# Weight loads, weight conversions and the last product's scaling stand at other steps in a relational graph layer

## The chip, the cores and the metric

The kernel runs on one core of one Trainium2 chip. The time is the device time of one execution in microseconds; lower is better. Before the change it is 1454.06 us, the median of 3 runs (1453.46 to 1455.05).

## What is computed

Two relational graph convolutions over 1250 nodes with 768 features and 21250 edges of 8 relations, then a residual and a layer norm. Each convolution takes the mean of the source rows for every pair of node and relation, multiplies it by the relation's matrix, sums over the relations and adds a root product and a bias:

```python
def _rgcn_conv(x, src, dst, etype, W, root, b):
    seg = dst * num_rel + etype
    sums = segment_sum(x[src], seg)                  # per (node, relation)
    cnt = segment_sum(ones, seg)
    mean = (sums / maximum(cnt, 1.0)[:, None]).reshape(num_nodes, num_rel, -1)
    return einsum('nri,rio->no', mean, W) + x @ root + b

h = relu(_rgcn_conv(x, src, dst, etype, W1, root1, b1))
out = _layernorm(x + _rgcn_conv(h, src, dst, etype, W2, root2, b2))
```

## The kernel before

The kernel turns the order round: it multiplies first, y = h W_r for all nodes, and then gathers rows of y by edge and sums them by destination. Every fp32 operand is cut in two parts that TensorE takes, a rounded one ("high") and the rest ("low"), and a product is three matmuls: high by high, high by low, low by high.

There are 18 products, numbered 0 to 17 here as `q` in the code: 0 to 7 are the relations of layer 1, 8 is its root; 9 to 16 and 17 are those of layer 2. A product has 20 steps: column half h = 0 with ten tiles of 125 nodes, then h = 1 with the same ten. A step is 6 x 3 = 18 matmuls of 128x384 into one of four PSUM banks. Of a product that is stored, ScalarE copies the bank to one of four slots of `y_stage` (`stage_y`), SyncE issues two DMAs that store it to y in HBM (`store_y`), and the slot is free for step s + 4 once both have landed (`y_stored[s % BANKS]`).

A "sum" (`bucket`) adds up one tile of 125 nodes of one relation. Its two row tiles (in the last relation of a layer four, of which the last is folded in half) are gathered from y by GpSimd (`gather_tile`, into seven, later five slots of `raw`), ScalarE makes `g_high` of each (`high_of_tile`; four slots, so a tile waits until TensorE has used the tile four before it), VectorE makes `g_low` (`cut_low`) and the one-hot matrix of destinations (`mark`), TensorE multiplies (8 matmuls for a plain sum, 14 for one of four row tiles), and VectorE adds the result to `acc` (`add`).

Products 4, 5 and 6 go with sums of two relations each ("pairs of sums"), one sum behind nearly every step. Product 7 and those of layer 2 go with sums of one relation. The root products 8 and 17 are written by `finish`: their 20 steps stay in PSUM, and the sums of the last relation of the layer are added onto them in the same banks.

Weights come in halves. `load_unit(q, h)` is one DMA of 1152 KB by SyncE into the single buffer `w_raw`; it waits until the half before has been converted. `high_of_unit` is its conversion on ScalarE, `low_of_unit` that on VectorE (in the pair products in two pieces, by the table `in_parts`). Half 1 of product q is needed at step 10, half 0 of q + 1 at its step 0. At which step each engine does this is written out by hand in three places: `relation` (SyncE; loads behind the stores of steps 8 and 14), `matrix` of ScalarE (steps 1 and 11) and `matrix` of VectorE (the table `low_at`). Each engine works in the order written: what stands behind a waiting instruction waits too. At step s of ScalarE the sum's `g_high` come first, then `stage_y(s)`, then the conversion. The kernel has no scheduler.

`finish(1)`, the last product, also does the layer norm. For tile t VectorE makes mean and variance (`moments_of`), ScalarE the root (`deviation`), VectorE its reciprocal and the shift (`scale_of`), and ScalarE scales the rows (`norm`), which SyncE stores to `out`. The last tile is done in two halves (`last_bucket`, `last_moments`) and scaled by VectorE.

Of the kernel before, what the change touches and what calls it, by code (L numbers as in the profile page):

```python
# [8 lines left out]
def rgcn_residual_layernorm(nc, x, src, dst, etype, w_all, b1, b2, out):  # L9
# [23 lines left out]
    K = D // P  # L33
# [51 lines left out]
    with ctx:  # L85
# [305 lines left out]
        def _(sp):  # L391
# [20 lines left out]

            def relation(q, yc, r):
                for s in range(STEPS):
                    store_y(yc, r, s)
                    if isinstance(q, int) and q == TABLE_END and s == 3:
                        sp.wait_ge(flags_counted, 1)
                        sp.dma_start(inv_table.rearrange("(p k) o -> p (k o)", p=P), inv_count[:])\
                            .then_inc(inv_stored, 16)
                    if s == 8:  # L420
                        load_unit(q + 1, 0)
                    if s == 14:
                        load_unit(q + 1, 1)

# [36 lines left out]
            for q in range(1, ROOT1):  # L461
                relation(q, q, q)
                if q == TABLE_END:
                    sp.wait_ge(bucket_added, 2 + T)
                    sp.dma_start(bias[:], b2.rearrange("(o n) -> o n", o=1).to_broadcast([P, D]))\
                        .then_inc(bias_loaded, 16)
# [146 lines left out]
        def _(act):  # L613
# [41 lines left out]

            def matrix(q, yc, actions=lambda s: [], after=None):


                for s in range(STEPS):
                    for what, g, _, t in actions(s):  # L660
                        if what == "sum":
                            bucket(g, t)
                    stage_y(yc, STEPS * q + s, s, bank_of(s))
                    for what, turn, _, t in actions(s):
                        if what == "turn":
                            high_of_turn(turn, t)
                    if s == 1:
                        high_of_unit(q, 1)
                    if s == 11:
                        high_of_unit(q + 1, 0)  # L670
                    if after:
                        after(s)
# [39 lines left out]
            def finish(layer):  # L712
# [5 lines left out]
                for t in range(T):  # L718
                    if layer == 0 and t == T - 2:
                        high_of_unit(q + 1, 0, STEPS * q + FIRST_HALF)  # L720
                    if t + 1 < T:
                        bucket(g, t + 1)
                    if layer == 0:
                        relu(t)
                        if t:
                            high_of_turn(1, t - 1)
                    else:
                        deviation(t)
                        if t + 1 < T:
                            norm(t)  # L730

# [11 lines left out]
            for q in range(TABLE_END, ROOT1 - 1):  # L743
                matrix(q, q, pair_of(q))
            matrix(ROOT1 - 1, ROOT1 - 1, one_relation(R - 2, None))
            finish(0)
# [235 lines left out]
        def _(dve):  # L982
# [372 lines left out]
            def finish(layer):  # L1355
# [6 lines left out]
                for t in range(T):  # L1362
                    if layer == 0 and t == T - 2:
                        low_of_unit(unit(q + 1, 0), 0)
                    if t + 1 < T:
                        cut_low(g, t + 1, 0, 1)
                    if (layer, t) == (1, T - 1):
                        last_moments(g, t)
                        continue
                    add(g, R - 1, t)  # L1370
                    if t + 1 < T:
                        cut_low(g, t + 1, 1)
                    if layer:
                        moments_of(t)
                    if t + 2 < T:
                        mark(g, R - 1, t + 2)
                    if layer and t + 1 < T:
                        scale_of(t)
                    elif layer == 0 and t:
                        low_of_turn(1, t - 1)  # L1380
# [23 lines left out]

            in_parts = ((4, 0, K // 2), (7, K // 2, K), (13, 0, K // 2), (16, K // 2, K))
            for q in range(TABLE_END, ROOT1 - 1):
# [35 lines left out]
```

## Time and profile before

| | us |
|---|---|
| median of 3 runs | 1454.06 |
| the profiled execution | 1466.17 |
| its span in the trace | 1464.3 |
| TensorE busy | 1437.1 (98%) |
| VectorE busy | 927.6 (63%) |
| ScalarE busy | 573.1 (39%) |
| GpSimd busy | 559.0 (38%) |

The profiled execution lies 12.1 us above the median of the runs, and 1.9 us of it lie outside the span. The trace knows the engines as PE (TensorE matmul), PEld (its weight load), DVE (VectorE), ACT (ScalarE), POOL (GpSimd) and SP (SyncE). In brackets behind a row of the timeline stand the idle time of the engine just before it and what ended that. PE is nearly always busy, so what can be won is in its few gaps and at the two ends.

### The profile page before, as it was taken

The page shows a single profiled execution, that of the slowest core. Times are in us where ns is not written, and L with a number is a line of the kernel's source. Part 1 is how long each engine was busy: PE and PEld are TensorE (multiplying, and loading weights), DVE is VectorE, ACT ScalarE, POOL GpSimd, SP SyncE. Part 2 cuts the span into 40 slices and gives each one's busy share as a digit, 9 for nine tenths or more (in the row PEclk, how much of TensorE's full clock was granted, in tenths as well). Part 3 has the DMA queues.
Part 4 walks back from the last instruction along what each step waited for, and adds up shares of the span by engine and source line. Part 5 has one row for each costly group of instructions (what it writes and reads, how often), then busy time and mean ns, then how long its engine had stood idle before and what let it go on. Part 6 is the DMA issues. An engine that isn't in the chain of part 4 may idle for free.

```text
span 1464.3 us, 23621 instructions
## 1 busy us (share of the span) xinstructions
PE 1437.1 (98%) x8715; PEld 1419.6 (97%) x8715; DVE 927.6 (63%) x1475; ACT 573.1 (39%) x805; POOL 559.0 (38%) x437
## 2 busy tenths in 40 slices
PE   8999999999999899999999999999999999999997
PEld 8999999999999899999999999999999999999996
DVE  7899999857777577456771154545454454444677
ACT  4222334335444444344552233333343333433454
POOL 0000000066777686425535232434242424243552
PEclk9999999999999999999999999999999999999998
DMA  6414321358877776664463465646464656656454
GB/s 195 152 60 127 96 72 47 106 183 267 254 211 227 227 229 191 212 200 149 136 189 103 148 211 168 210 144 218 142 211 156 199 177 184 194 171 213 119 169 123
DMA packets 112523, 248.58 MB, mean 170 GB/s; under 512 B 19617, under 2 KB 87768, under 8 KB 112446
## 3 DMA queue, kind: packets, MB, share of 16 engines
q0 software_dynamic: 30880, 134.67, 31.1%
q1 hardware_dynamic: 81566, 112.88, 24.1%
q8 instruction: 48, 0.79, 0.2%
q14 instruction: 29, 0.24, 0.0%
HBM read 192.77 MB, written 65.49 MB: 176 GB/s over the span
## 4 chain that ended last, share of the span: by engine, by line
PE 89%; DVE 6%; issue 3%; ACT 1%; DMA 1%; SPq 0%; ACTq 0%; POOLq 0%
PE prod L767 70%; PE agg L809 14%; DVE g_low L1029 2%; PE agg L904 2%; PE agg L767 2%; PE prod L809 1%; PE agg L758 1%; DVE g_high L1029 1%; ACT g_high L628 1%; DVE acc L1046 1%; DVE g_low L1033 1%; DMA x_rows<-in_x 0%; PE agg L907 0%; DVE stats L1401 0%; DMA raw<-y,bucket_index 0%
## 5 line engine op out<-in xcount | busy, mean ns | idle before, releaser
L767 PE MATMUL prod<-w_high,h_high 128*128 128x384 f32 x2064 | 693.5, 336 | 0.0
L767 PE MATMUL prod<-w_high,h_low 128*128 128x384 f32 x2064 | 690.4, 335 | 0.0
L767 PE MATMUL prod<-w_low,h_high 128*128 128x384 f32 x2064 | 690.1, 334 | 0.0
L519 POOL DMA_INDIRECT raw<-y,bucket_index x310 | 410.5, 1324 | 538.5 <-DVE g_low L1033 220.1
L653 ACT ACTIVATE y_stage<-prod 128x384 f32<-128x384 f32 x320 | 157.7, 493 | 781.6 <-PE prod L767 631.1
L1033 DVE TENSOR_TENSOR g_low<-raw,g_high 128x768 fp32r<-128x768 f32 x240 | 220.4, 956 | 370.6 <-ACT g_high L631 312.4
L767 PEld LDWEIGHTS prod<-w_high,h_high 128*128 128x128 f32 x2064 | 388.1, 188 | 0.1
L767 PEld LDWEIGHTS prod<-w_low,h_high 128*128 128x128 f32 x2064 | 388.0, 188 | 0.0
L767 PEld LDWEIGHTS prod<-w_high,h_low 128*128 128x128 f32 x2064 | 387.8, 188 | 0.0
L631 ACT ACTIVATE g_high<-raw 128x768 fp32r<-128x768 f32 x240 | 189.9, 839 | 1.9 <-DMA raw<-y,bucket_index 1.5
L809 PE MATMUL agg<-g_high,one_hot 128*128 128x384 f32 x616 | 159.8, 340 | 10.1 <-DVE g_low L1033 7.6
L809 PE MATMUL agg<-g_low,one_hot 128*128 128x384 f32 x602 | 153.5, 336 | 0.0
L1049 DVE SCALAR_TENSOR_TENSOR acc<-agg,inv_count,acc 128x768 f32<-128x768 f32 x130 | 131.7, 1013 | 11.4 <-PE agg L809 7.6
L809 PEld LDWEIGHTS agg<-g_high,one_hot 128*128 128x128 f32 x616 | 109.8, 189 | 16.3 <-issue 13.7
L995 DVE TENSOR_TENSOR w_low<-w_raw,w_high 128x2304 fp32r<-128x2304 f32 (+1 forms) x43 | 92.8, 2158 | 33.7 <-ACT w_high L619 32.0
L578 POOL MEMSET raw<- 128x3840 f32 x1 | 3.3, 3310 | 288.0 <-PE agg L907 288.0
L809 PEld LDWEIGHTS agg<-g_low,one_hot 128*128 128x128 f32 x602 | 109.3, 189 | 0.0
L1017 DVE TENSOR_SCALAR one_hot<-column,dst_local 128x128 fp32r<-128x128 bf16 x360 | 86.8, 305 | 0.5
L519 POOL DMA_INDIRECT x_rows<-y,bucket_index x50 | 67.2, 1344 | 34.5 <-DVE g_low L1033 18.7
L1029 DVE SCALAR_TENSOR_TENSOR g_low<-raw,scale,g_high 128x768 fp32r<-128x768 f32 x52 | 51.4, 1014 | 41.8 <-ACT g_high L628 31.0
L628 ACT ACTIVATE g_high<-raw,scale 128x768 fp32r<-128x768 f32 x70 | 60.6, 927 | 43.2 <-issue 24.5
L619 ACT ACTIVATE w_high<-w_raw 128x2304 fp32r<-128x2304 f32 x35 | 74.4, 2124 | 1.1 <-PE agg L767 0.6
(179 smaller groups left out, 992.7 us busy)
## 6 DMA issues: line engine op xcount, KB each, us to landing
y<-y_stage SPq DMA_DIRECT2D x320, 168.0 KB
w_raw<-in_w_all SPq DMA_DIRECT2D x35, 1152.0 KB
y<-y_stage SPq DMA_DIRECT2D x320, 19.5 KB
raw<-y,bucket_index POOLq DMA_INDIRECT x310
acc<-in_x POOLq DMA_DIRECT2D x10, 375.0 KB, 6.4
x_rows<-in_x SPq DMA_DIRECT2D x10, 336.0 KB
out<-acc SPq DMA_DIRECT2D x10, 336.0 KB
w_raw<-in_w_all SPq DMA_DIRECT2D x2, 576.0 KB, 4.6
```

Source lines behind the costliest of these rows:

```text
L519: pool.indirect_dma_start(raw_rows(slot), None, y[0:written * N, :], bass.IndirectOffsetOnAxis(ap=bucket_index[:, at_column:at_column + 1] ...
L619: act.activation(w_high[:, h], w_raw[:], ACT.Copy).then_inc(w_high_ready, 1)
L628: act.activation(g_high[:, split_slot(g, i), :], raw_rows(slot), ACT.Copy, scale=scale[:, column:column + 1])\
L631: act.activation(g_high[:, split_slot(g, i), :], raw_rows(slot), ACT.Copy).then_inc(high_ready, 1)
L653: act.activation(y_stage[:, s % BANKS, :], prod[:, bank, 0:HALF], ACT.Copy)\
L767: mm = pe.matmul(to, left[:, k, t * P:(t + 1) * P], right[:, h, k, :], start=(k == 0 and left is h_high and right is w_high), stop=(n == 0 ...
L809: mm = pe.matmul(to[:, c, :], one_hot[:, par, b, :], part[:, split_slot(g, i), c * HALF:(c + 1) * HALF], start=(onto is None and b == 0 an ...
L995: ins = dve.tensor_tensor(w_low[:, h, part], w_raw[:, part], w_high[:, h, part].bitcast(f32), ALU.subtract)
L1017: ins = dve.tensor_scalar(one_hot[:, par, b, :], column[:], dst_local[:, bass.ds(column_of(r, t, b), 1)], None, ALU.is_equal)
L1029: ins = dve.scalar_tensor_tensor(low[p:P, split_slot(g, i), :], rows, scale[p:P, at_scale:at_scale + 1], high, ALU.mult, ALU.subtract)
L1033: ins = dve.tensor_tensor(low[p:P, split_slot(g, i), :], rows, high, ALU.subtract)
L1049: ins = dve.scalar_tensor_tensor(a, agg[:, t % 2, :, 0:HALF], inv_count[:, bass.ds(r * T + t, 1)], onto, ALU.mult, ALU.add)
```

## The change

Four numbers per pair product move, and two engines' order in the last product:

- SyncE, products 4, 5 and 6: the loads of product q + 1 stand behind the stores of steps 9 and 17, not 8 and 14.
- ScalarE, the same products: the conversions stand at steps 3 and 12, not 1 and 11; in product 7 at 2 and 11, not 1 and 11.
- VectorE, the same products: the first piece of each half stands at steps 5 and 14, not 4 and 13; the second pieces stay at 7 and 16.
- Last product: root and scaling of tile t - 1 are done in round t, not those of tile t. On ScalarE the first `g_high` of the next tile goes ahead of the root and the scaling goes behind the other three; on VectorE `scale_of(t - 1)` stands right behind `add(t)`.

```diff
-                    if s == 8:
-                        load_unit(q + 1, 0)
-                    if s == 14:
-                        load_unit(q + 1, 1)
+                    if s in load_at:
+                        load_unit(q + 1, load_at.index(s))
...
-                relation(q, q, q)
+                relation(q, q, q, (9, 17) if TABLE_END <= q < ROOT1 - 1 else (8, 14))
...
-                matrix(q, q, pair_of(q))
-            matrix(ROOT1 - 1, ROOT1 - 1, one_relation(R - 2, None))
+                matrix(q, q, pair_of(q), high_at=(3, 12))
+            matrix(ROOT1 - 1, ROOT1 - 1, one_relation(R - 2, None), high_at=(2, 11))
...
-                    if t + 1 < T:
-                        bucket(g, t + 1)
+                    rows = list(enumerate(tile_range(g, t + 1))) if t + 1 < T else []
+                    for b, i in rows[:1]:
+                        high_of_tile(g, i, tiles(g) * (t + 1) + b)
+                    if layer and t:
+                        deviation(t - 1)
+                    for b, i in rows[1:]:
+                        high_of_tile(g, i, tiles(g) * (t + 1) + b)
                     if layer == 0:
                         relu(t)
...
-                    else:
-                        deviation(t)
-                        if t + 1 < T:
-                            norm(t)
+                    if layer and t:
+                        norm(t - 1)
+                if layer:
+                    deviation(T - 1)
...
                     if (layer, t) == (1, T - 1):
+                        scale_of(t - 1)
                         last_moments(g, t)
                         continue
                     add(g, R - 1, t)
+                    if layer and t:
+                        scale_of(t - 1)
...
-                    if layer and t + 1 < T:
-                        scale_of(t)
-                    elif layer == 0 and t:
+                    if layer == 0 and t:
...
-            in_parts = ((4, 0, K // 2), (7, K // 2, K), (13, 0, K // 2), (16, K // 2, K))
+            in_parts = ((5, 0, K // 2), (7, K // 2, K), (14, 0, K // 2), (16, K // 2, K))
```

How it moves instructions, at three places. First SyncE's queue in product 5, around the second load. `y<-y_stage` are the two stores of one step. Before, the load is behind the stores of step 14:

```order
L409 DMA y<-y_stage 13x384
L402 DMA w_raw<-in_w_all 128x6x384 [waits w_low_ready,w_high_ready]
L409 DMA y<-y_stage 112x384 [waits y_staged]
L409 DMA y<-y_stage 13x384
L409 DMA y<-y_stage 112x384 [waits y_staged]
```

Now the same rows stand six rows further down, and the six are the stores of steps 15 to 17, which came behind the load before.

Second, ScalarE in product 5 at steps 11 and 12. Before:

```order
L653 ACTIVATE y_stage<-prod 128x384 [waits y_stored3,prod_done]
L619 ACTIVATE w_high<-w_raw 128x2304 [waits prod_done,w_loaded]
L631 ACTIVATE g_high<-raw 128x768 [waits tile_used,raw_loaded1]
L631 ACTIVATE g_high<-raw 128x768 [waits tile_used,raw_loaded2]
L653 ACTIVATE y_stage<-prod 128x384 [waits y_stored0,prod_done]
```

Now:

```order
L651 ACTIVATE y_stage<-prod 128x384 [waits y_stored3,prod_done]
L629 ACTIVATE g_high<-raw 128x768 [waits tile_used,raw_loaded1]
L629 ACTIVATE g_high<-raw 128x768 [waits tile_used,raw_loaded2]
L651 ACTIVATE y_stage<-prod 128x384 [waits y_stored0,prod_done]
L617 ACTIVATE w_high<-w_raw 128x2304 [waits prod_done,w_loaded]
```

The conversion of the weights (`w_high`) has moved behind the next sum's two `g_high` and behind the copy of step 12.

Third, ScalarE at the end of the last product; `std` is `deviation`, `acc<-acc,shift,std` is `norm`. Before, the rounds that make the last two tiles' `g_high`, and the end:

```order
L738 ACTIVATE acc<-acc,shift,std 128x768 [waits norm_ready]
L628 ACTIVATE g_high<-raw,scale 128x768 [waits scale_loaded,tile_used,raw_loaded1]
L628 ACTIVATE g_high<-raw,scale 128x768 [waits scale_loaded,tile_used,raw_loaded2]
L628 ACTIVATE g_high<-raw,scale 128x768 [waits scale_loaded,tile_used,raw_loaded3]
L628 ACTIVATE g_high<-raw,scale 128x768 [waits scale_loaded,tile_used,raw_loaded4]
L734 ACTIVATE std<-moments,eps 128x1 [waits var_ready]
L738 ACTIVATE acc<-acc,shift,std 128x768 [waits norm_ready]
L734 ACTIVATE std<-moments,eps 128x1 [waits var_ready]
```

Now:

```order
L626 ACTIVATE g_high<-raw,scale 128x768 [waits scale_loaded,tile_used,raw_loaded1]
L737 ACTIVATE std<-moments,eps 128x1 [waits var_ready]
L626 ACTIVATE g_high<-raw,scale 128x768 [waits scale_loaded,tile_used,raw_loaded2]
L626 ACTIVATE g_high<-raw,scale 128x768 [waits scale_loaded,tile_used,raw_loaded3]
L626 ACTIVATE g_high<-raw,scale 128x768 [waits scale_loaded,tile_used,raw_loaded4]
L741 ACTIVATE acc<-acc,shift,std 128x768 [waits norm_ready]
L737 ACTIVATE std<-moments,eps 128x1 [waits var_ready]
L741 ACTIVATE acc<-acc,shift,std 128x768 [waits norm_ready]
```

The root that stands among the last tile's `g_high` is now that of the tile two before it, and no scaling stands ahead of them. Number, kind and size of the instructions are the same on every engine, and TensorE's and GpSimd's order is unchanged.

## Rows read from the trace of the kernel before

**Rows 1.** The page: span, and PE's granted clock in 40 slices (tenths)

```profile
span 1464.3 us, 23621 instructions
...
PEclk9999999999999999999999999999999999999998
```

**Rows 2.** Timeline, PE's gaps: start, us, engine, line, operation [idle before, releaser]

```profile
315.53 0.58 PE L809 MATMUL agg<-g_high,one_hot 128*128 128x384 f32 x2 [1.29 <-DVE g_low L1033]
...
460.86 0.59 PE L809 MATMUL agg<-g_high,one_hot 128*128 128x384 f32 x2 [0.72 <-issue]
466.79 0.58 PE L809 MATMUL agg<-g_high,one_hot 128*128 128x384 f32 x2 [1.04 <-DVE g_low L1033]
...
604.96 0.61 PE L809 MATMUL agg<-g_high,one_hot 128*128 128x384 f32 x2 [0.87 <-issue]
```

**Rows 3.** Timeline, SyncE's queue in product 5, second weight load

```profile
464.94 2.61 SPq L409 DMA_DIRECT2D y<-y_stage  x4
481.55 0.40 SPq L402 DMA_DIRECT2D w_raw<-in_w_all  x1
482.00 0.98 SPq L409 DMA_DIRECT2D y<-y_stage  x2
```

**Rows 4.** Timeline, VectorE: second piece of the low weights

```profile
480.13 1.35 DVE L995 TENSOR_TENSOR w_low<-w_raw,w_high 128x1152 fp32r<-128x1152 f32 x1
```

**Rows 5.** Timeline, ScalarE at steps 18 and 19 of product 5 and 0 of 6

```profile
485.21 0.50 ACT L653 ACTIVATE y_stage<-prod 128x384 f32<-128x384 f32 x1 [2.55 <-PE prod L767]
...
495.64 0.49 ACT L653 ACTIVATE y_stage<-prod 128x384 f32<-128x384 f32 x1 [8.47 <-issue]
...
497.75 0.49 ACT L653 ACTIVATE y_stage<-prod 128x384 f32<-128x384 f32 x1 [0.16 <-DMA y<-y_stage]
```

**Rows 6.** Timeline, the matmul in which PE's longest gap ends

```profile
498.00 0.66 PE L809 MATMUL agg<-g_high,one_hot 128*128 128x384 f32 x1 [3.81 <-DVE g_low L1033]
```

**Rows 7.** Chain of work behind that gap: start, us, what

```profile
498.00 2.90 PE agg L809 x8
500.90 4.42 PE prod L767 x18
...
506.71 3.12 PE prod L767 x18
509.83 1.65 PE agg L809 x8
```

**Rows 8.** Timeline, ScalarE: conversion at step 1 of product 4

```profile
311.54 2.12 ACT L619 ACTIVATE w_high<-w_raw 128x2304 fp32r<-128x2304 f32 x1
```

**Rows 9.** Timeline, ScalarE's copy of step 12 of product 5

```profile
458.50 0.49 ACT L653 ACTIVATE y_stage<-prod 128x384 f32<-128x384 f32 x1 [3.66 <-remote]
```

**Rows 10.** Timeline, ScalarE: last two rounds of the last product

```profile
1448.81 1.03 ACT L738 ACTIVATE acc<-acc,shift,std 128x768 f32<-128x768 f32 x1 [0.76 <-DVE shift L1385]
1449.75 3.40 ACT L628 ACTIVATE g_high<-raw,scale 128x768 fp32r<-128x768 f32 x4
```

**Rows 11.** Chain of work at the end: one round and the last steps

```profile
1440.67 0.93 ACT g_high L628
1441.63 1.02 DVE g_low L1029
...
1447.51 0.21 DVE moments L1403
...
1457.57 0.47 DVE acc L1394
...
1460.48 0.68 DVE acc L1418
```

**Rows 12.** Waits of PE's weight load from 1386 to 1450 us: total, times, longest

```profile
PEld prod L809 <- DVE g_high L1029: 2.0, 5, 0.4
PEld agg L809 <- DVE g_high L1029: 0.8, 2, 0.4
```

**Rows 13.** Timeline, PE: first matmul of tile 8's sum

```profile
1444.05 0.33 PE L809 MATMUL prod<-g_high,one_hot 128*128 128x384 f32 x1
```

More of the change, by code:

```diff
@@ L411, in store_y, with relation @@
                                  y_stage[rows, s % BANKS, :]).then_inc(y_stored[s % BANKS], 16)
-            def relation(q, yc, r):
+            def relation(q, yc, r, load_at=(8, 14)):
                 for s in range(STEPS):
@@ L654, in stage_y, with matrix @@
                     .then_inc(y_staged, 1)
-            def matrix(q, yc, actions=lambda s: [], after=None):
+            def matrix(q, yc, actions=lambda s: [], after=None, high_at=(1, 11)):
                 for s in range(STEPS):
@@ L666, in matrix @@
                             high_of_turn(turn, t)
-                    if s == 1:
+                    if s == high_at[0]:
                         high_of_unit(q, 1)
-                    if s == 11:
+                    if s == high_at[1]:
                         high_of_unit(q + 1, 0)
@@ L720, in finish @@
                         high_of_unit(q + 1, 0, STEPS * q + FIRST_HALF)
-                    if t + 1 < T:
-                        bucket(g, t + 1)
+                    rows = list(enumerate(tile_range(g, t + 1))) if t + 1 < T else []
[5 more added lines that the diff above has]
+                        high_of_tile(g, i, tiles(g) * (t + 1) + b)
                     if layer == 0:
                         relu(t)
-                        if t:
-                            high_of_turn(1, t - 1)
-                    else:
-                        deviation(t)
-                        if t + 1 < T:
-                            norm(t)
+                    if layer == 0 and t:
+                        high_of_turn(1, t - 1)
+                    if layer and t:
+                        norm(t - 1)
+                if layer:
+                    deviation(T - 1)
             def deviation(t):
@@ L1376, in finish @@
                         mark(g, R - 1, t + 2)
-                    if layer and t + 1 < T:
-                        scale_of(t)
-                    elif layer == 0 and t:
+                    if layer == 0 and t:
                         low_of_turn(1, t - 1)
```

## The prediction

> **What bounds the kernel now.** I read the page first: the span is 1464.3 us, TensorE's granted clock stands at 9 tenths or more in all 40 slices but the last [rows 1], and TensorE is busy 98% of it. No edit touches a matmul, so the change can only shorten TensorE's gaps, a stretch at half clock that follows one of them, and what comes behind its last matmul. I therefore read the timeline for PE rows that carry an idle time, then went back from each to the engine that was late, and last read the chain of waits through the final product.
>
> Gaps in reach of the pair-product edits: 1.29 us at the start of product 4; 0.72 and 1.04 us in product 5 behind steps 13 and 14, which come again in product 6; 0.87 us in product 7 [rows 2]; and the largest, 3.81 us, at the start of product 6 [rows 6].
>
> The 3.81 us gap reads as follows. SyncE issues four DMAs, the stores of steps 13 and 14, by 467.6, then nothing until the weight load at 481.55 [rows 3]. It waits there because the load may start only when the half before is converted, and VectorE's last piece runs from 480.13 to 481.48 [rows 4]. The stores of steps 15 to 17 are written behind the load and wait with it; the first goes out at 482.00 [rows 3]. Step 19 needs the slot of step 15, and ScalarE gets it only at 495.64, 8.47 us idle; step 0 of product 6 gets that of step 16 at 497.75 [rows 5]. The `g_high` of the next sum stands behind that copy, so TensorE's sum starts at 498.00. Then the clock is at half for a while: the 8 matmuls of that sum take 2.90 us and the next 18 take 4.42, against 3.12 for 18 at full clock [rows 7]. At 3.12 / 18 = 0.173 us a matmul, 8 are 1.39, so the stretch costs 1.51 + 1.30 = 2.8 us more. The place costs 3.8 + 2.8 = 6.6 us.
>
> In the last product ScalarE makes the next tile's `g_high` only after root and scaling of this one: the scaling starts at 1448.81, the four `g_high` at 1449.75 [rows 10]. The round is 1449.75 - 1440.67 = 9.08 us [rows 10, 11], while TensorE's own work in it is two steps and one sum, 50 matmuls, 8.67 us. The rest is the wait for the folded row tile, 2.8 us in 7 rounds [rows 12]. So this product is a closed loop of ScalarE and VectorE, by a narrow margin.
>
> **The change, part by part.**
>
> Second load behind step 17. What it waits for does not move (VectorE's piece at step 16), so the load itself still goes out near 481.5. Steps are 4.5 us apart here and step 18 is copied at 485.21 [rows 5], so step 17's store is ready at about 481.2, before the load. The stores of steps 15 to 17 no longer wait, and step 19 finds its slot free. Gain: between 0 and 6.6 us. It is 0 if the median run has no such gap, which I can't exclude: the profiled execution is 12.1 us above the median, and a gap made by a DMA's landing is the kind that may differ. At the two like transitions, into products 5 and 7, the trace has no PE gap of this kind at all. I take the gap without the clock, 3.8 us, and keep both ends.
>
> First load behind step 9, conversion at step 12. Both go one step later, so the load has the same time to land. Cost 0; the cover is the 8 steps until product q + 1 begins.
>
> Conversion at step 3 instead of 1. In product 4 it takes 2.12 us from 311.54 [rows 8], right ahead of the first pair of `g_high`, and TensorE waits 1.29 us [rows 2]. Moved, those go first. A conversion in the steady loop costs TensorE little: behind the one at step 1 of product 6 the sum takes 1.65 us instead of 1.39 [rows 7], 0.3. Product 4: -1.3 + 0.3 = -1.0 us. Products 5 and 6: the same 0.3 one place further. In product 7 the conversion moves right ahead of the first sum: by the durations above the first `g_low` is ready some 1.3 us after TensorE wants it, against the gap of 0.87 [rows 2], so +0.4.
>
> The gaps behind steps 13 and 14 of products 5 and 6. ScalarE's copy of step 12 starts at 458.50, 3.66 us idle, with a releaser that the profile can't name [rows 9], though the matmuls of that step end some 3 us earlier; the sum behind it is late for that. Nothing says whether this hangs on the conversion at step 11. Bounds: 0, and -2 x (0.72 + 1.04) = -3.5 us. It could also grow. I take 0, as I can't name what would take it away.
>
> Last product, rounds. With the first `g_high` ahead of the root and the scaling of the tile before behind the rest, the loop is open. From the first `g_low` to the end of mean and variance VectorE works 1447.72 - 1441.63 = 6.1 us [rows 11], with the scale 6.5, with the one-hot tiles about 7.3; that is under 8.67. The wait goes: -2.8 us. Bounds 0 and -2.8.
>
> Last product, end. Tile 8's sum begins at 1444.05 [rows 13] (now 2.8 earlier, counted above) and all ends at 1461.16 [rows 11]. In the new order the first `g_high` of tile 9 may start once TensorE has used tile 8's first row tile, 0.7 us in, and ends 0.93 us later [rows 11], at 1445.7. VectorE then works 6.5 us to the end of tile 8's mean and variance: 1452.2. Root, reciprocal and shift take about 0.9 us: 1453.1. TensorE's last sum is done by then: it can start at 1444.05 + 2.43 + 3.12 = 1449.6, and its last `g_low` is ready at about 1450.9. From the last tile's first addition to the end are 1461.16 - 1457.57 = 3.6 us [rows 11]: 1456.7. Gain 4.4 us. The store of tile 8 goes out before that of tile 9, as now. Bounds 0, if the gathers of tile 9 are what is late, and -4.4.
>
> Sum of what both executions must have: -1.0 + 0.4 - 2.8 - 4.4 = -7.8 us. With the store gap -7.8 - 3.8 = -11.6 us. Against the profiled execution that is 1466.2 - 11.6 = 1454.6; I put the same difference on the median: 1454.1 - 11.6 = 1442.5 us.
>
> **The rivals.**
>
> Only the last product and product 4 gain, since the unprofiled runs have no store gap: 1454.1 - 7.8 = 1446.3. For it speak the 12.1 us between profile and median; against it that SyncE's wait for VectorE follows from the written order.
>
> All gaps go, clock included: -7.8 - 6.6 - 3.5 = -17.9, so 1436.2. For it speaks that the gaps of products 5 and 6 repeat alike, so they hang on the order of work, which changes there; against it that no rule for them can be read.
>
> The last product keeps its length, since gathers for the earlier `g_high` come late. With the store gap gone: -1.0 + 0.4 - 3.8 = -4.4, so 1449.7; with it staying: 1453.5. Against it: each gather is issued when VectorE has freed its slot, and VectorE's work for a tile moves ahead with the rest.
>
> Slower: the stores that now stand behind the load hold up step 2 of the next product. The store of step 18 goes out at about 485.7, behind the load. The store of step 16, out at about 483.0 behind the load, held its slot until 497.75 [rows 5], nearly 15 us. Without the gap step 2's product ends at about 503.2. So the store of step 18, landing by 500.5, has under 3 us to spare; this decides as soon as it takes over 17.5 us. If it does at all three transitions, each costs what the one costs now: 3 x 6.6 - 6.6 = +13.2, with the rest -7.8 it is +5.4, so 1459.5 us.
>
> The Trainium skill, in "DMA: Bandwidth & Descriptors", section "Queues, rings and completion order", says that descriptors on one ring of SyncE's queue are consumed in ring order, and that each DMA engine takes turns between queues. By that rule the store of step 18 can't overtake the load and the gathers slow both, which is this rival; the 8.47 us in [rows 5] agree with it, and the place in the queue of steps 15 to 17 is what the same rule gives back.
>
> **How the numbers follow.** Chances: forecast 0.60; last product alone 0.14; all gaps 0.12; last product keeps its length 0.09, of which 0.04 with the store gap gone; slower 0.05. About 0.2%, 2.9 us, is what a measurement of this kernel can tell from no change. Faster by more: 0.60 + 0.14 + 0.12 + 0.04 = 0.90; within: 0.05; slower: 0.05. The range runs from 1435 to 1447.5: it takes in the forecast with both ends of the store gap, the last product alone and all gaps, 0.86 in all.
>
> **What would show it.** Right: in the trace after, SyncE's stores of steps 15 to 17 go out 4.5 us apart before the second load; ScalarE's copy of step 19 follows its product at once; no half clock before the last few us; TensorE's rounds in the last product 8.7 us and no wait for the folded tile; the first gap of product 4 gone. Wrong: a late copy at step 2 of a product after a pair product, gaps at step 3 or 12 with an unnamed releaser, ScalarE waiting for `raw` in the last product, or the end of the last addition less than 3 us nearer to tile 8's sum.

## The result, and the profile after

The changed kernel takes 1445.12 us, the median of 4 runs (1444.87 to 1447.08), beside 1454.03 us for the kernel before (4 runs, 1453.46 to 1455.05). The ratio is 0.994, 95% interval 0.992 to 0.996: 8.9 us faster. The forecast was 1442.5 us, its range 1435 to 1447.5.

The two profiled executions differ by far more, 1464.3 against 1443.3 us of span. Where that lies is told by the lengths of the products, from the end of TensorE's last matmul of one to that of the next. "Control" is a second execution of the kernel before, from the first set of experiments below:

| us | before | control | after |
|---|---|---|---|
| products 0 to 3 | 304.7 | 305.2 | 304.0 |
| product 4 | 91.60 | 91.61 | 89.86 |
| product 5 | 93.39 | 91.17 | 90.67 |
| product 6 | 99.84 | 91.29 | 90.67 |
| product 7 | 77.43 | 76.27 | 77.94 |
| products 8 to 16 | 692.3 | 692.1 | 692.1 |
| product 17, the last | 91.01 | 91.10 | 87.99 |
| behind its last step | 14.05 | 14.04 | 10.11 |
| span | 1464.3 | 1452.7 | 1443.3 |

So 11.6 of the 21 us are what the profiled execution of before had more than the control, nearly all of it in products 5 to 7. Of the other 9.4, 3.1 + 3.9 = 7.0 us are the last product's, 1.75 product 4's, 0.5 + 0.6 products 5 and 6, and product 7 takes 1.67 more. That makes 8.2 us. The last 1.2 us lie in products 0 to 3, which no edit touches; their length goes from 303.7 to 306.5 us over the traces of this document, so it is no part of the change.

The page of the changed kernel, its first line and its clock:

```profile
span 1443.3 us, 23621 instructions
...
PEclk9999999999999999999999999999999999999999
```

The clock stands at 9 tenths or more in the last slice too, where [rows 1] have 8.

The timeline of SyncE's queue, product 5, which answers to [rows 3]:

```profile
462.54 14.28 SPq L409 DMA_DIRECT2D y<-y_stage  x8
476.92 0.40 SPq L402 DMA_DIRECT2D w_raw<-in_w_all  x1
480.57 18.79 SPq L409 DMA_DIRECT2D y<-y_stage  x10
```

The row `x8` joins the eight DMAs from 462.54 on, the stores of steps 14 to 17; they go out one step after the other, and no store waits behind the load. It leaves at 476.92, the store of step 18 at 480.57. VectorE's second piece, which answers to [rows 4]:

```profile
474.97 1.34 DVE L998 TENSOR_TENSOR w_low<-w_raw,w_high 128x1152 fp32r<-128x1152 f32 x1
```

ScalarE's copies of steps 18 and 19 of product 5 and 0 and 1 of product 6 (timeline; compare [rows 5]):

```profile
480.05 0.49 ACT L651 ACTIVATE y_stage<-prod 128x384 f32<-128x384 f32 x1 [2.55 <-PE prod L770]
...
484.56 0.49 ACT L651 ACTIVATE y_stage<-prod 128x384 f32<-128x384 f32 x1 [2.54 <-PE prod L770]
...
489.06 0.49 ACT L651 ACTIVATE y_stage<-prod 128x384 f32<-128x384 f32 x1 [2.55 <-PE prod L770]
...
493.57 0.49 ACT L651 ACTIVATE y_stage<-prod 128x384 f32<-128x384 f32 x1 [2.54 <-PE prod L770]
```

Each is released by its own product, 4.5 us apart, where step 19's copy came after 8.47 us in [rows 5].

Product 7, where the time got longer: ScalarE's conversion at step 2, the first pair of `g_high` behind it, and the first matmul of the first sum on TensorE:

```profile
586.36 2.12 ACT L617 ACTIVATE w_high<-w_raw 128x2304 fp32r<-128x2304 f32 x1
588.38 1.56 ACT L629 ACTIVATE g_high<-raw 128x768 fp32r<-128x768 f32 x2
...
590.35 0.59 PE L812 MATMUL agg<-g_high,one_hot 128*128 128x384 f32 x2 [1.29 <-DVE g_low L1036]
```

This is the gap that product 4 had in [rows 2], with the same 1.29 us; in product 4 it is gone. It has moved to the product whose conversion now stands right ahead of the first sum.

ScalarE in one round of the last product and at its end (timeline; L626 `g_high`, L737 root, L741 scaling; compare [rows 10]):

```profile
1419.74 0.94 ACT L626 ACTIVATE g_high<-raw,scale 128x768 fp32r<-128x768 f32 x1 [4.14 <-issue]
1420.59 0.28 ACT L737 ACTIVATE std<-moments,eps 128x1 f32<-128x1 f32 x1
1420.77 2.58 ACT L626 ACTIVATE g_high<-raw,scale 128x768 fp32r<-128x768 f32 x3
1423.26 1.02 ACT L741 ACTIVATE acc<-acc,shift,std 128x768 f32<-128x768 f32 x1
1428.41 0.94 ACT L626 ACTIVATE g_high<-raw,scale 128x768 fp32r<-128x768 f32 x1 [4.14 <-issue]
```

The round is 1428.41 - 1419.74 = 8.67 us, TensorE's own work. What TensorE's weight load waits for from 1372 us on (total, times, longest; compare [rows 12]), then tile 8's sum (compare [rows 13]) and the chain of work at the end (compare [rows 11]):

```profile
PEld agg L825 <- DVE g_high L1032: 0.6, 1, 0.6
```

```profile
1427.47 0.51 PE L812 MATMUL prod<-g_high,one_hot 128*128 128x384 f32 x2
```

```profile
1428.41 0.95 ACT g_high L626
...
1435.57 0.22 DVE moments L1407
...
1439.47 0.68 DVE acc L1422
```

The waits for the folded tile in the rounds are gone; one of 0.6 us is left in the last sum. From tile 8's sum to the end of the last row of the chain are 1440.15 - 1427.47 = 12.7 us, against 17.1 in [rows 11, 13].

### The profile page after: what moved, and what is told of

Read it like the earlier page. It is cut to its first block, busy times and chain, and to the rows that moved or that the text cites. A ratio compares the mean times of both kernels' runs of the same rounds, so it can differ in the third digit from the quotient of the medians.

```text
span 1443.3 us, 23621 instructions
## 1 busy us (share of the span) xinstructions
PE 1427.0 (99%) x8715; PEld 1416.2 (98%) x8715; DVE 926.7 (64%) x1475; ACT 572.3 (40%) x805; POOL 553.0 (38%) x437
## 4 chain that ended last, share of the span: by engine, by line
PE 95%; DVE 1%; issue 1%; DMA 1%; ACT 0%; POOL 0%; SPq 0%; POOLq 0%; ACTq 0%
PE prod L770 73%; PE agg L812 14%; PE agg L770 3%; PE agg L907 2%; PE prod L812 2%; PE agg L761 1%; DVE g_low L1032 1%; DMA x_rows<-in_x 0%; PE agg L910 0%; POOL raw L517 0%; DMA raw<-y,bucket_index 0%; DVE g_high L1032 0%; ACT g_high L626 0%; DVE acc L1049 0%; ACT w_high L617 0%
## 5 line engine op out<-in xcount | busy, mean ns | idle before, releaser
L517 POOL DMA_INDIRECT raw<-y,bucket_index x310 | 403.4, 1301 | 523.1 <-DVE g_low L1036 216.6
L626 ACT ACTIVATE g_high<-raw,scale 128x768 fp32r<-128x768 f32 x70 | 61.7, 928 | 70.1 <-issue 50.0
```

The costliest lines, as they stand in the source:

```text
L517: pool.indirect_dma_start(raw_rows(slot), None, y[0:written * N, :], bass.IndirectOffsetOnAxis(ap=bucket_index[:, at_column:at_column + 1] ...
L626: act.activation(g_high[:, split_slot(g, i), :], raw_rows(slot), ACT.Copy, scale=scale[:, column:column + 1])\
```

## The experiments

Each run of a kernel stands beside runs of the kernel before on the same chip, and they were made in three sets on different chips. The kernel before took 1452.6 us (median, 1451.8 to 1455.3) in the first set, 1458.5 us (1455.2 to 1464.0) in the second and 1452.9 us (1451.7 to 1457.3) in the third. So differences are read within a set, and where two sets are put side by side the text says so.

### First set: was the gap there, and what does each part bring

The profiled execution of before, 12.1 us above the median, had carried the argument. First the same kernel again, with no edit.

> The kernel before, unchanged, to see what a second execution of it shows. Theory A (the 3.81 us gap at the start of product 6 and the half clock behind it belong to the one profiled execution): a span near 1452, no gap above 1.5 us at the start of product 6, product 6 as long as product 5 or shorter (about 91 to 93.4 us, not 99.8). Theory B (the gap is in every execution, and the changed kernel pays for it elsewhere): a span near 1464 and product 6 at 99.8 us again.

Measured: 1454.6 us, span 1452.7. Theory A holds for this execution. What SyncE, ScalarE and TensorE do at the end of product 5, from the control's timeline:

```profile
479.82 0.40 SPq L402 DMA_DIRECT2D w_raw<-in_w_all  x1
480.26 18.59 SPq L409 DMA_DIRECT2D y<-y_stage  x14
...
490.30 0.49 ACT L653 ACTIVATE y_stage<-prod 128x384 f32<-128x384 f32 x1 [4.87 <-DMA y<-y_stage]
...
492.67 0.59 PE L809 MATMUL agg<-g_high,one_hot 128*128 128x384 f32 x2 [0.21 <-DVE g_low L1033]
```

The wait is there: the stores of steps 15 to 17 stand behind the load, and step 19's copy waits for the slot until 490.30, 2.4 us after its product. But TensorE is idle for 0.21 us, not 3.81. Counted from the issue of the load, the slot came free after 490.30 - 479.82 = 10.5 us here and after 495.64 - 481.55 = 14.1 us in the profiled execution of before [rows 3, 5]. There the copy was 6.0 us late and TensorE idle for 3.81, so some 2.2 us of lateness cost TensorE nearly nothing.

The last product's part alone (`finish` of ScalarE and VectorE as changed, all else as before):

```diff
-                    if t + 1 < T:
-                        bucket(g, t + 1)
+                    rows = list(enumerate(tile_range(g, t + 1))) if t + 1 < T else []
+                    for b, i in rows[:1]:
+                        high_of_tile(g, i, tiles(g) * (t + 1) + b)
+                    if layer and t:
+                        deviation(t - 1)
...
                     add(g, R - 1, t)
+                    if layer and t:
+                        scale_of(t - 1)
```

> The kernel before with the last product's part alone (root and scaling one tile back on ScalarE and VectorE). Two traces give 93.0 less for this part: the last product 91.01 to 87.99 us, -3.0, and from its last step to the end 14.05 to 10.11 us, -3.9. Theory A: -7.0 in the median, so a ratio of 0.995. Theory B (part of this gain is lent by the pairs' part, by gathers that run earlier): under 4 us, 0.997 or more.

(The "93.0 less" in it is a slip of the pen: the figures behind it are meant.) Measured: 1445.39 us against 1452.62, -7.2 us, ratio 0.995 (0.994 to 0.996). The last product takes 88.01 us and 10.11 lie behind it. Theory A: the part needs no help from the other.

The pair products' part alone:

```diff
-                relation(q, q, q)
+                relation(q, q, q, (9, 17) if TABLE_END <= q < ROOT1 - 1 else (8, 14))
...
-                matrix(q, q, pair_of(q))
-            matrix(ROOT1 - 1, ROOT1 - 1, one_relation(R - 2, None))
+                matrix(q, q, pair_of(q), high_at=(3, 12))
+            matrix(ROOT1 - 1, ROOT1 - 1, one_relation(R - 2, None), high_at=(2, 11))
...
-            in_parts = ((4, 0, K // 2), (7, K // 2, K), (13, 0, K // 2), (16, K // 2, K))
+            in_parts = ((5, 0, K // 2), (7, K // 2, K), (14, 0, K // 2), (16, K // 2, K))
```

> The kernel before with the pair products' part alone (the loads of weights, the conversions, the low pieces, and the conversion of product 7). Theory A: what is left of the median's -8.9 us behind the last product's -7.0, so about -2 us: -1.7 in product 4, up to -0.7 in products 5 and 6 together, +0.5 in product 7; ratio 0.9985 to 0.9995, while its span against the profiled one of before is 13 us shorter. Theory B: -9 us or more in the median, ratio 0.993 or less.

Measured: 1452.20 us against 1452.62, -0.4 us, ratio 0.999 (0.998 to 1.000), less than expected and not told from nothing. The trace against the control: product 4 -1.73, 5 -0.47, 6 -0.59, 7 +1.67, so -1.1 in all. The expectation had product 7 at +0.5, which is what it reads against the profiled execution of before, and that one had a gap of 0.87 us of its own there [rows 2].

The loads alone, at (9, 17):

```diff
-                relation(q, q, q)
+                relation(q, q, q, (9, 17) if TABLE_END <= q < ROOT1 - 1 else (8, 14))
```

> The kernel before with SyncE's loads behind steps 9 and 17 in products 4 to 6, and nothing else. Theory A: no store waits behind the second load any more, so no late copy at steps 19 and 0 in the trace, but the median moves by less than 1 us, since a usual execution has no gap there to take away. The gaps behind steps 13 and 14 of products 5 and 6 (0.7 to 1.0 us each) tell more: if they stay, they hang on the conversion at step 11, which stands as before; if they go, on the loads. Theory B: -6.6 us or more in the median.

Measured: 1457.27 us (1453.3 to 1461.9), ratio 1.002 (1.001 to 1.003). That is a loss, which neither theory had. As theory A has it, no copy of steps 19 and 0 is late, and no gap stands behind steps 13 and 14 either. The loss is at step 12. In product 5, SyncE, ScalarE and TensorE, from the timeline:

```profile
443.11 0.40 SPq L402 DMA_DIRECT2D w_raw<-in_w_all  x1
...
454.53 2.12 ACT L617 ACTIVATE w_high<-w_raw 128x2304 fp32r<-128x2304 f32 x1 [4.39 <-DMA w_raw<-in_w_all]
...
458.52 0.98 PE L807 MATMUL agg<-g_high,one_hot 128*128 128x384 f32 x2 [4.40 <-DVE g_low L1031]
```

The load goes out at 443.11 and its last part lands when ScalarE's conversion at step 11 begins, 11.4 us later. ScalarE waits 4.39 us for it, the next sum's `g_high` stand behind, and TensorE is idle for 4.40 us; in product 6 the same place has 2.31 us. The control's load of this half goes out at 439.52 and its conversion starts at 452.05 without a wait. So the first load can't stand one step later with its conversion left at step 11; in the changed kernel the conversion moves along, and nothing waits for the load. The traced execution is the slowest of the 11 runs, so these gaps are an upper end.

### Second set: the last product's mechanism, product 7, and the loads

ScalarE's part of the last product alone: the diff of the last product without its second piece, so `scale_of(t)` stays at the end of VectorE's round t.

> The kernel before with ScalarE's part of the last product alone; VectorE still does reciprocal and shift of tile t at the end of round t, so it waits there for a root that ScalarE makes only behind the next tile's first g_high. Theory C (what closed the loop was ScalarE's order alone, and VectorE has time to spare): in the trace with the whole part VectorE is idle 1.5 us before each first g_low and the root ends 0.2 us after that g_high, so the first g_low moves back by about 0.6 us and TensorE does not feel it: the last product 88.0 us, behind its last step 10.1 to 10.8 us, median -6.4 to -7.0 us, ratio 0.995 to 0.9956. Theory D (VectorE's wait stands in for ScalarE's): TensorE waits for the folded row tile in each round again, the last product 90 to 91 us, median -4 us or less, ratio 0.997 or more.

Measured: 1451.77 us against 1458.54, -6.8 us, ratio 0.995 (0.994 to 0.997). The last product takes 88.01 us, 10.30 lie behind. Theory C. VectorE at the start of a round, from its timeline:

```profile
1433.36 0.17 DVE L1389 RECIPROCAL std<-std 128x1 f32<-128x1 f32 x1 [1.52 <-ACT std L739]
1433.56 0.21 DVE L1390 TENSOR_SCALAR shift<-moments,std 128x1 f32<-128x1 f32 x1
1433.69 1.01 DVE L1034 SCALAR_TENSOR_TENSOR g_low<-raw,scale,g_high 128x768 fp32r<-128x768 f32 x1
```

VectorE waits for the root, as the order says, but it has the time: with the whole part it stands idle as long in the same place, ahead of the first `g_low`. The wait costs 0.2 us once, at the end. VectorE's edit on top of ScalarE's is worth no more than that; ScalarE's order was what closed the loop. VectorE's edit without ScalarE's was not run.

The changed kernel with one number put back:

```diff
-            matrix(ROOT1 - 1, ROOT1 - 1, one_relation(R - 2, None), high_at=(2, 11))
+            matrix(ROOT1 - 1, ROOT1 - 1, one_relation(R - 2, None), high_at=(1, 11))
```

> The changed kernel with one number put back: product 7's first conversion at step 1, not 2. Product 7 took 76.27 us in a trace of the kernel before without the gaps of the profiled one, and 77.94 us with the conversion at step 2, where it stands right ahead of the first sum's g_high and TensorE waits 1.5 us. Theory E (that conversion costs 1.67 us and nothing is won by it): product 7 at 76.3 us, 1.6 us off the time of the changed kernel, ratio to the kernel before 0.9928. Theory F (the load of this half, now issued at step 17 of product 6, lands too late for a conversion at step 1): the conversion waits for its load, and the time is that of the changed kernel or above; the load was issued at 567.6 and landed at 573.4, and step 1 is copied at 582.85, so 9 us speak against it.

Measured: 1447.26 us against 1458.54, ratio 0.992 (0.990 to 0.994). Product 7 takes 76.27 us: the conversion at step 1 has landed weights and nobody waits. The changed kernel itself was not in this set, so it is compared in the third. Against the kernel before the gain is 11.3 us, where theory E's ratio of 0.9928 stands for 10.5; the interval, 8 to 15 us, can't tell them apart.

The same trace shows that the pair products' part does not make products 5 and 6 safe. ScalarE, copy of step 14 of product 5, from the timeline:

```profile
465.79 0.49 ACT L651 ACTIVATE y_stage<-prod 128x384 f32<-128x384 f32 x1 [6.65 <-remote]
```

It starts 3.9 us after its product, TensorE is idle for 1.72 us behind step 15, and product 5 takes 94.3 us, not 90.7.

The conversions and low pieces without the loads (the part of the pair products, with `(9, 17)` back at `(8, 14)`):

> The kernel before with ScalarE's conversions and VectorE's low pieces at their new steps, the loads at 8 and 14 as before. Theory G (each part does its own): product 4 -1.7 us as with the whole pair part, products 5 and 6 as in the control or slightly above (91.2 and 91.3), since the stores of steps 15 to 17 still wait behind the second load; product 7 +1.67; sum 0 to +0.3 us, ratio 1.000. Theory H (the first load at 8 and the conversion at 12 give the landing 4.5 us more, and this is worth something in the usual execution): -1 us or more.

Measured: 1457.57 us against 1458.54, ratio 0.999 (0.998 to 1.001). Product 4 takes 89.91 us and product 7 77.91, as both theories say. So the conversions can move without the loads. The copy of step 14 of product 5 is 5.4 us late and product 5 takes 95.6. Between G and H it decides nothing: late copies weigh more than what the theories differ by.

The second load alone at 17, the first at 8:

```diff
-                relation(q, q, q)
+                relation(q, q, q, (8, 17) if TABLE_END <= q < ROOT1 - 1 else (8, 14))
```

> The kernel before with the second load behind step 17 and the first at 8 as before. With both moved (9, 17) the median rose by 4.65 us, and in that trace the conversion at step 11 of product 5 waited 4.4 us for the first load. Theory G (all of that loss is the first load's; the second load gives its little gain): no late copy at steps 12, 19 and 0, products 5 and 6 at 90.7 us each, 1.0 us off the control, ratio 0.9990 to 0.9996. Theory H (a part of the loss is the second load's): slower than before, products 5 and 6 above 91.5 us.

Measured: 1458.29 us against 1458.54, ratio 1.000 (0.998 to 1.001). The 0.2% of loss with both loads moved is absent, although on another chip, and with the 4.40 us wait for the first load above this puts the loss on that load, as theory G has it. The rest of theory G is not borne out: its gain of 1 us is not seen, and products 5 and 6 take 91.73 and 91.83 us, above the 91.5 that theory H named. The copies of steps 19 and 0 are on time in the trace, those of step 12 of product 5 (0.3 us) and steps 4 and 5 of product 6 (2.3 and 2.9 us) are late.

### Third set: dose, bytes, and the two versions side by side

The changed kernel again, with no edit:

> The changed kernel, unchanged, beside the next run on the same chip. So far its parts alone gave -7.2 us (last product) and -0.4 us (pair products) where the kernel before takes 1452.6 us. Theory E: on any chip at least -7.6 us, ratio 0.9948 or less, and more where the kernel before has late copies in products 5 and 6. A ratio above 0.996 would say that the parts take from each other.

Measured: 1445.56 us against 1452.92, -7.4 us, ratio 0.995 (0.994 to 0.996). Theory E had at least -7.6 us, ratio 0.9948 or less: the median misses it by 0.2 us, and the bound lies in the interval. The parts' -7.2 and -0.4 us come from the first set's chip, and the -0.4 was not told from nothing there. As far as that goes the parts add up; the ratio is below the 0.996 that would have said that they take from each other.

> The changed kernel with product 7's first conversion back at step 1, on the same chip as the changed kernel. Theory E: 1.6 us below it, product 7 at 76.3 us. Theory F: equal to it or above.

Measured: 1444.48 us (1443.2 to 1445.4) against 1445.56 (1444.8 to 1446.4) for the changed kernel and 1452.92 for the one before, ratio to before 0.994 (0.993 to 0.996). By the medians it is 1.1 us faster than the changed kernel, by the traces 77.91 - 76.27 = 1.64 us in product 7; the intervals of the two ratios overlap, but four of its five runs are faster than all five of the changed kernel. ScalarE in product 7, from the timeline:

```profile
584.20 2.12 ACT L617 ACTIVATE w_high<-w_raw 128x2304 fp32r<-128x2304 f32 x1
586.93 0.49 ACT L651 ACTIVATE y_stage<-prod 128x384 f32<-128x384 f32 x1 [0.61 <-PE prod L770]
587.32 1.58 ACT L629 ACTIVATE g_high<-raw 128x768 fp32r<-128x768 f32 x2
```

The conversion ends before step 2's copy, and the first pair of `g_high` has nothing ahead of it. This is the fastest version of this set.

The second load one step earlier than before, so that more stands behind it:

```diff
-                relation(q, q, q)
+                relation(q, q, q, (8, 13) if TABLE_END <= q < ROOT1 - 1 else (8, 14))
```

> The kernel before with the second load behind the stores of step 13, not 14, in products 4 to 6: one step's stores more stand behind a load that waits for VectorE's piece at step 16. Theory K (stores behind the waiting load are what makes copies late, and the rest of the time a slack of some 2 us hides it): in the control the load goes out at 479.8 and the stores behind it let the copy of step 19 begin at 490.30, 2.4 us late, with a gap on TensorE of 0.1 us. Step 18's copy, due at 483.5, would wait for a store landing near 490, 6.5 us late, so TensorE loses some 4.3 us at each of three transitions, with a clock loss behind it up to 7: +13 to +20 us, ratio 1.009 to 1.014. Theory L (late landings at the end of a product come from gathers and the load's bytes, not from the order in the queue): under +3 us.

Measured: 1464.19 us against 1452.92, +11.3 us, ratio 1.008 (1.006 to 1.009). SyncE, ScalarE and TensorE at the end of product 5, from the timeline:

```profile
483.52 0.40 SPq L402 DMA_DIRECT2D w_raw<-in_w_all  x1
483.96 12.40 SPq L409 DMA_DIRECT2D y<-y_stage  x12
...
493.24 0.49 ACT L651 ACTIVATE y_stage<-prod 128x384 f32<-128x384 f32 x1 [8.61 <-DMA y<-y_stage]
...
495.60 0.67 PE L807 MATMUL agg<-g_high,one_hot 128*128 128x384 f32 x2 [3.95 <-DVE g_low L1031]
```

The copy of step 18 is 6.1 us late (6.5 were expected) and TensorE is idle for 3.95 us (4.3). The transition into product 5 has 3.7 us too, that into product 7 only 1.25, which is why the total lies below the 13 to 20 us. Theory K: the order in SyncE's queue is the mechanism, and one step's stores are the difference between hidden and not. The granted clock behind that gap, beside a stretch without one (the window, its length, the busy time of PE, PEld, DVE, ACT and POOL, then PEclk, DMA share, GB/s):

```profile
470.00:480.00 10.00, 10.00 (x59) 10.00 (x59) 7.34 (x13) 4.91 (x8) 7.87 (x8) 1.00 0.66 184
495.00:505.00 10.00, 9.40 (x45) 9.43 (x46) 7.57 (x13) 4.00 (x7) 7.09 (x6) 0.83 0.61 172
```

The last kernel halves the bytes of the weight loads that products 5 to 7 use. It leaves out the other half of the weights, so the buffer keeps older numbers there; the number and size of the conversions and matmuls stay:

```diff
-                sp.dma_start(w_raw[:], w).then_inc(w_loaded, 16)
+                k = K // 2 if isinstance(q, int) and TABLE_END < q < ROOT1 else K
+                sp.dma_start(w_raw[:, 0:k], w[:, 0:k]).then_inc(w_loaded, 16)
```

> The kernel before, with the loads that products 5, 6 and 7 use cut to half their bytes (576 KB each; the second half of the buffer keeps older numbers, so this part of the products is left wrong; conversions and matmuls stay in number and size). Asked is what makes some copies late at steps 12 to 14 of products 5 and 6 in some executions (0.7 to 2.4 us of gap each) and spreads the kernel before between 1452 and 1466 us. Theory M (the weight load's bytes hold back the stores around it in the queue): late copies at steps 12 to 14 and 19 gone, products 5 and 6 at 91.2 us or less, the median near 1451.5 us and the runs within 2 us. Theory N (the gathers hold back the stores, with or without the load): the spread and the late copies stay, ratio 0.998 or more.

Measured: 1452.38 us against 1452.92, ratio 1.000 (0.999 to 1.001); its 11 runs lie within 1.3 us (1451.9 to 1453.2), the 15 runs of before within 5.5. No copy of products 5 and 6 is late and both take 90.67 us. ScalarE's copies of steps 18 and 19 of product 5:

```profile
481.71 0.49 ACT L654 ACTIVATE y_stage<-prod 128x384 f32<-128x384 f32 x1 [2.54 <-PE prod L768]
486.21 0.49 ACT L654 ACTIVATE y_stage<-prod 128x384 f32<-128x384 f32 x1 [2.54 <-PE prod L768]
```

With the load's order as before but half its bytes, the stores behind it land in time: of the lateness at step 19 theory M is right. Of steps 12 to 14 the run decides nothing. The median is 0.9 us above the 1451.5 that theory M gave, and the ratio lies above the 0.998 that theory N gave. On this chip the kernel with the second load at 13, whose loads have all their bytes, has no late copy at steps 12 to 14 either. And the narrow spread may be step 19's: the changed pair products with whole loads, which have no late copy at step 19, spread by 1.5 us over 11 runs in the first set.

## Why the prediction was right, and where its terms were off

The time lies in the range, 2.6 us above the forecast, and the sign is right. But the case that the measurement comes nearest to is the first rival, the last product and product 4 alone (1446.3 us), which had a chance of 0.14, not the forecast with its 0.60. The measured 8.9 us are 2.7 short of the forecast's 11.6, and it is the width of the range, 12.5 us, that takes them in: the range is right, its middle is not. By terms:

- **Second load, -3.8 us: the step that failed, mis-sized.** The mechanism is real: it is in the control, and a load one step earlier makes it cost 11 us. Its size was read from one execution that lay 12.1 us above the median. In a usual one the gap on TensorE is 0.2 us, and products 5 and 6 win 0.5 + 0.6 us. The prediction had named this bound, 0, and the reason for it, and still took the trace's value because the wait follows from the written order. The wait does; its price depends on when the store lands, 10.5 us behind the issue of the load in one execution and 14.1 in another, and the first 2.2 us of lateness are slack.
- **Product 4, -1.0 us: measured -1.75.** Both gaps ahead of its first two sums, 1.29 and a shorter one behind it, went, and the 0.3 us that I charged for the conversion at its new step was not paid.
- **Product 7, +0.4 us: measured +1.67.** The lateness of 1.3 us was worked out right; the row of after says 1.29, and a shorter gap follows. From it I took off the 0.87 us gap of [rows 2], which was a relic of the late stores at the end of product 6: GpSimd's first gather of the next relation waits for the last of these stores and starts at 596.21, 3.5 us behind the copy of step 19, which is itself 3.1 us late; ScalarE then waits 1.53 us for a gathered tile at 603.06. The control has no gap there, and its product 7 takes 76.27 us.
- **Gaps behind steps 13 and 14, 0 us.** The value was right for a usual execution, which has no such gaps. The rows could say more than I read in them. The copy of step 12 waits for its product and for the landing of step 8's store; the product was done, so it was the store. That store is one of the four DMAs of the first row here, ahead of the load in the queue, not behind it (SyncE, timeline of before):

```profile
433.36 5.27 SPq L409 DMA_DIRECT2D y<-y_stage  x4
438.72 0.40 SPq L402 DMA_DIRECT2D w_raw<-in_w_all  x1
```

It was out by 438.63, and the copy got its slot at 458.50, 19.9 us later; a place behind the load can't be the cause of this one. The page of before gives the loads of weights and the gathers no time from issue to landing, where the control has 6.8 and 4.9 us: landing records are missing there, and a wait for a landing then may bear "remote" or "issue" as its releaser. The suspicion against the conversion falls: with ScalarE's part of the last product alone, whose conversion stands at step 11, the copies of steps 13 and 14 of product 5 were 2.4 and 3.7 us late, and with the conversion at step 12 those same copies were 1.6 and 5.4 us late, on one chip.
- **Rounds of the last product, -2.8 us: -2.5** from the product's start to tile 8's sum (84.8 to 82.3 us). **End, -4.4 us: -4.4** from tile 8's sum to the last addition's end (17.1 to 12.7 us). Together that is the -7.0 of the table, which cuts at another place. This term was worked out duration by duration along the new order, and it held. None of the rows of its last round and end waits for the landing of a DMA.
- **Slower by the store of step 18 behind the load:** did not come. No copy of steps 0 to 2 behind a pair product is late in either trace of the changed kernel.

The Trainium skill, in "DMA: Bandwidth & Descriptors", section "Queues, rings and completion order", says that descriptors on one ring are consumed in ring order and that a DMA engine takes turns between the queues that have work for it. The traces agree with the first: two stores behind a whole load gave their slot free 10.5 us after the load went out, and with half the load's bytes ahead of them the slot was free when its product was done, 8.2 us after the load (478.05 to 486.21). No run here tells the second apart, since the gathers were never changed alone. It was right to weigh that rule as a rival, and the store of step 18 had more room than I had worked out: the copy of step 2 is on time in both traces of the changed kernel.

What stays open is why stores land late in the middle of products 5 and 6 in some executions. In three of the four traces of the second set copies of steps 13 to 15 of product 5 are late, in two of the four those of steps 4 and 5 of product 6. The latter wait for the stores of steps 0 and 1, which go out more than 11 us behind the last weight load, so that load's bytes are a poor explanation for them. One thing goes with it. The page gives no time from issue to landing for the weight loads and the gathers in five traces, that of before and the four of the second set, and these five are the ones with such late copies; in none of the other nine traces are records missing in this way or a copy of these steps late, other than those behind a late conversion in the run with both loads moved. Whether the two have one cause no run shows. A run of half the bytes on the chip that shows the late copies was not made.

## What to carry to other kernels

If the profiled execution lies above the median by more than the change is worth, a gap in it that hangs on a DMA's landing is priced at the slack it overruns, not at its row; take the lower bound, or a second execution. A DMA that must wait for something belongs behind all stores that are ready before it, and a load should not move later without the conversion that waits for it: both loads moved without the conversions made the kernel 4.6 us slower, by the wait for the first of them. Where an engine serves a loop it should do what the next round waits for first, and the remainder of the last round behind it; that gain was the one that could be computed from durations alone.

## What the runs showed of the hardware

A gap of TensorE costs more than its length once it is long. Behind the idle time of 3.95 us above, the granted clock is 0.83 on the mean of 10 us, so part of it was at the lower of the two levels, 1.2 and 2.4 GHz. In the chain of work of the same kernel, from 495 us:

```profile
495.60 2.59 PE agg L807 x8
498.19 3.73 PE prod L765 x18
501.92 1.39 PE agg L807 x8
```

8 matmuls take 2.59 us and then 1.39, and 18 take 3.73 where [rows 7] have 3.12 at full clock: 1.2 and 0.6 us more. [rows 7] show 2.8 in all behind 3.81 us. A shorter gap can do it too. Behind the 1.72 us in product 5 of the changed kernel with product 7's conversion at step 1, on the chip of the second set (chain of work, then the window as above):

```profile
468.15 1.86 PE agg L812 x8
470.01 4.57 PE prod L770 x18
```

```profile
468.00:478.00 10.00, 9.85 (x47) 9.72 (x48) 8.63 (x14) 3.55 (x6) 8.20 (x6) 0.83 0.58 166
```

That is 0.5 and 1.4 us more, so the gap of 1.72 us costs 3.6; product 5 takes 94.32 us there, 3.65 above the 90.67 of the changed kernel. Behind the 1.29 us of product 7 in the changed kernel the granted clock is 1.00 on the mean of 10 us, and the 18 matmuls of the next step take 3.13 us.

The spread of the same kernel from chip to chip, 1452.6 to 1458.5 us in the medians, is larger than the whole pair products' part, and larger than I had expected of a kernel whose TensorE is busy 98% of the span.
